# Clearing a stage's semaphores by ranges of numbers instead of one by one

## What is computed

```python
# x: (1, 2048, 256), ctx: (1, 1601, 256)
x = x + L0_xattn(ln(x), ctx, Wq, Wk, Wv, Wo, bo, Wfc, gamma, beta)
x = x + L0_ffn(ln(x), router_w, expert_bias, w1, w3, w2, sw1, sw3, sw2)
x = x + L1_xattn(ln(x), ctx, ...)        # attention both ways and a gate
x = x + L1_ffn(ln(x), gate_W, expert_W, out_W)

# L0_ffn: 8 experts, the 2 best for each token, and 2 shared experts
shared = sum(ffn(xf, sw1[i], sw2[i], sw3[i]) for i in range(2))
rw, sel = top_k(xf @ router_w.T + expert_bias, 2)
rw = softmax(rw)
out = shared + sum(combine[:, e] * ffn(xf, w1[e], w2[e], w3[e]) for e in range(8))
# ffn(x, w1, w2, w3) = (silu(x @ w1.T) * (x @ w3.T)) @ w2.T
```

## Time and profile before

| | us |
|---|---|
| median of 3 runs | 1076.73 |
| lowest and highest | 1076.3, 1080.12 |
| the profiled execution | 1076.45 |
| its span, first to last instruction | 1074.5 |

### The profile page before, as it was taken

One profiled execution on the slowest core, in us unless ns is written; L12 is line 12 of the kernel. 1 busy time (PEld: TensorE's weight loads), 2 busy tenths in 40 slices (PEclk: granted clock), 3 DMA queues, 4 the chain that ended last, 5 costly groups with the idle time before them and its releaser, 6 DMA issues. The chain is left out here.

```text
span 1074.5 us, 18717 instructions
## 1 busy us (share of the span) xinstructions
PE 998.5 (93%) x6840; PEld 919.0 (86%) x6840; DVE 678.7 (63%) x1605; ACT 512.2 (48%) x1041; POOL 404.3 (38%) x636
## 2 busy tenths in 40 slices
PE   4999999599999999999889999999999999999983
PEld 4899998478889999997778799998998999999973
DVE  5567776359668888774675545455445677766662
ACT  4546665233367777772344433333334444444441
POOL 5225544415324343414542100000015867677540
PEclk9999999689999999999998999999999999999995
DMA  7200000021078888863213400000001101111000
GB/s 223 79 1 2 1 2 1 1 79 59 20 229 254 255 250 254 252 210 113 74 40 99 109 1 20 1 1 1 2 1 21 25 21 31 26 31 31 11 10 11
DMA packets 56881, 76.54 MB, mean 71 GB/s; under 512 B 5536, under 2 KB 37408, under 8 KB 56800
## 3 DMA queue, kind: packets, MB, share of 16 engines
q1 hardware_dynamic: 38896, 50.04, 15.7%
q0 software_dynamic: 15648, 22.81, 7.3%
q10 hardware_dynamic: 2256, 2.62, 0.7%
HBM read 61.43 MB, written 14.02 MB: 70 GB/s over the span
## 5 line engine op out<-in xcount | busy, mean ns | idle before, releaser
L43 PE MATMUL bank<-V_hi,XT_lo 128*128 128x256 f32 x416 | 123.6, 297 | 1.4 <-DVE XT_lo L2231 1.4
L2231 DVE TENSOR_TENSOR XT_lo<-bank,XT_lo 128x512 fp32r<-128x512 f32 x116 | 73.3, 633 | 76.3 <-ACT XT_lo L1924 75.8
L1924 ACT ACTIVATE XT_lo<-bank 128x512 fp32r<-128x512 f32 x116 | 63.8, 552 | 118.8 <-PE bank L1683 118.1
L45 PE MATMUL bank<-V_hi,XT_lo 128*128 128x256 f32 x416 | 117.1, 282 | 0.0
L44 PE MATMUL bank<-V_lo,XT_lo 128*128 128x256 f32 x416 | 116.8, 281 | 0.0
L454 DVE TENSOR_TENSOR expert_w_lo<-sraw,expert_w_hi 128x1024 fp32r<-128x1024 f32 x72 | 88.1, 1224 | 32.6 <-ACT expert_w_hi L450 30.2
L2236 DVE TENSOR_REDUCE part<-wide 128x1 f32<-128x402 f32 (+1 forms) x116 | 72.4, 624 | 38.7 <-PE wide L45 36.7
L43 PE MATMUL wide<-expert_w_hi,XT_hi 128*128 128x402 f32 (+1 forms) x232 | 91.5, 394 | 3.4 <-issue 2.4
L45 PE MATMUL wide<-expert_w_hi,XT_hi 128*128 128x402 f32 (+1 forms) x232 | 85.6, 369 | 0.0
L44 PE MATMUL wide<-expert_w_lo,XT_hi 128*128 128x402 f32 (+1 forms) x232 | 85.5, 368 | 0.0
L43 PEld LDWEIGHTS bank<-V_hi,XT_lo 128*128 128x128 f32 x416 | 78.3, 188 | 4.6 <-DVE XT_lo L2231 2.9
(11 more groups left out here) (454 smaller groups left out, 3242.9 us busy)
## 6 DMA issues: line engine op xcount, KB each, us to landing
sraw<-w1T SPq DMA_DIRECT2D x25, 512.0 KB, 5.0
sraw<-w3T SPq DMA_DIRECT2D x25, 512.0 KB, 5.1
sraw<-w2T SPq DMA_DIRECT2D x25, 512.0 KB, 6.9
XT_hi<-queries POOLq DMA_DIRECT2D x16, 256.0 KB, 3.2
routed_results<-rys POOLq DMA_DIRECT2D x15, 256.0 KB
X<-x ACTq DMA_DIRECT2D x4, 512.0 KB, 8.0
token_rows<-Fx SPq DMA_DIRECT2D x4, 512.0 KB, 4.9
out<-X SPq DMA_DIRECT2D x16, 128.0 KB, 1.7
```

The costliest lines, as they stand in the source:

```text
L43: pe.matmul(out, wh, xh, start=first, stop=False)
L45: return pe.matmul(out, wl, xh, start=False, stop=last)
L1924: act.activation(weights(g, nk, 0), transposed(g, nk), ACT.Copy).then_inc(sem["high"], 1)
L2231: dve.tensor_tensor(weights(g, nk, 1), transposed(g, nk), weights(g, nk, 0).bitcast(F32), ALU.subtract).then_inc(sem["low"], 1)
```

## The change

`give_back` is registered once for each stack instead of once for each call of `sems`, gets all semaphores that the stage took, sorts their numbers, and clears each run of consecutive numbers by one instruction. The instruction is the same as before, a clear of a range with a first and a last number; before, first and last were always equal.

```diff
+        taken_by = {}
+
         def sems(ctx, names):
             got = [free_sems.pop(0) for _ in names.split()]
 
-            def give_back():
-                for s in got:
-                    nc.gpsimd.sem_clear(s)
-                free_sems.extend(got)
-            ctx.callback(give_back)
+            def give_back(taken):
+                numbers = sorted(s.num for s in taken)
+                firsts = [n for n in numbers if n - 1 not in numbers]
+                lasts = [n for n in numbers if n + 1 not in numbers]
+                for first, last in zip(firsts, lasts):
+                    nc.gpsimd.sem_clear(range(first, last + 1))
+                free_sems.extend(taken)
+            if ctx not in taken_by:
+                taken_by[ctx] = []
+                ctx.callback(give_back, taken_by[ctx])
+            taken_by[ctx].extend(got)
             return got
```

## The result

The changed kernel takes 1069.19 us (median of 8 runs, 1067.3 to 1075.34), the kernel before 1076.8 us (8 runs on the same chip, 1074.53 to 1080.12). The ratio is 0.9932, with a 95% interval of 0.991 to 0.9953: 7.3 us less, between 5.1 and 9.7. The profiled run of the changed kernel took 1068.18 us.

A forecast was written before the change was run, and what follows sets the result against it. PE was busy 93%, but POOL's clears counted at the end and ahead of the closing stage: 6.0 + 1.92 = 7.9 us off 1076.45 gave 1068.53, predicted as 1068.6 us, range 1067.4 to 1071.6.

The forecast's parts named there:

- The tail: Program's end, where nothing but clears runs: 86 clears become 5, so 81 x 74 ns = 6.0 us leave the span.
- the term for the new instruction: All six places: each range clear costs 74 ns, however long its range; seven of them lie on the path.
- B: Rival at all clears: a clear walks its range at 44 ns a member; gain only 3.2 us, 1073.3 us; chance 0.08.
- The closing stage: Stage after the routed one: 28 clears become 2, POOL starts 1.92 us sooner and everything behind moves by 1.92 us.
- the string: Closing stage: POOL's store, gathers and inverse(0), started at the barrier, set the time of PE's transposes; SHIFT 1.92 us sooner.
- The wait at the transposes: Closing stage: PE's two waits, 3.43 us together, become one of about 1.5 us at the first transposes.
- Everything behind moves by 1.92: Closing stage: all work behind PE's wait at the first transposes comes 1.92 us earlier.
- The other four places: First attention, router, routed and last stages: fewer clears gain 0, with 0.3 us either way.
- A: Rival: the closing stage's gain fails through a slow start behind the barrier or a slipped landing; 1069.4 to 1070.5 us; chance 0.10.
- The sign that I had named for A: Closing stage's first product to the last stage's: 77.7 us forecast; still 79.6 us would mean its gain failed.
- C: Rival at the program's end: other engines' work hides the 6.0 us, only 1.92 remains; 1074.6 us; chance 0.05.
- D: Rival: a range costs above 74 ns a member, so the kernel is slower; 1078.3 us at 88 ns; chance 0.02.

The follow-up runs named there:

- the kernel with two edits: The changed kernel, with the last routed result's store moved to SP's queue and inverse(0) into the middle of the fourth group of gathers: 1067.4 us, ratio 0.9929.

## Why the prediction was right, and where it was off

**The tail: right in kind, 0.4 us too large.** 6.0 us predicted, 5.63 found. The 74 ns per single clear held (and held when doubled). What was off is the term for the new instruction: I took 74 ns each whatever the length, the five take 0.74 us in all instead of 0.37. "A range instruction that walks would be of little use" was the weak sentence: it walks, at 5.3 ns where issuing one more clear costs 74, and is of use all the same. B was right in form and 8 times too dear at 44 ns. The figure that it took from the Trainium skill ("Runtime: NRT & Kernel Launch", section "The ~15µs preamble/postamble breakdown": about 1.5 us for 51 semaphores), 29 ns each by my estimate, fits neither: here the trace has 74 for a clear by itself and 5.3 inside a range, and the measurement decides.

**The closing stage: the string was right, the size nearly at POOL, less so in the stage.** 1.92 us predicted for POOL's start, 1.71 found (the two ranges of 14 take 110 ns each). At SHIFT it was 1.76 in the mean of four against four. The steps up to SHIFT were seen: the store at 0.74 (0.6 to 0.7 predicted), the wait ahead of `result(1, 0)` gone in all four profiles with ranges. The wait at the transposes was not the 1.5 us predicted but 2.1 to 2.4 in three profiles and none in one. In the kernel with ranges in the closing stage alone PE came 1.29 us sooner to the transposes (34.14 against 35.43), where I had reckoned with 1.02, and SHIFT came 1.6 sooner, not 1.92; the difference, 0.6, is the longer wait.

**What the prediction did not have: the clock behind that wait.** "Everything behind moves by 1.92" took the products behind the transposes as fixed. They take 41.4 to 41.7 us or 42.8 to 43.3, by the granted clock, in kernels of both kinds. It fell in two of four profiles with single clears and in three of four with ranges (the fourth had no wait there), too few to say that the change made it more likely. The stage gained 1.4 us in the means, not 1.92, and the 1.4 leans on one profile.

**The other four places: right.** Nothing to be seen with ranges, nothing to be seen with twice the clears. Over the twelve profiles, six with single clears ahead of these stages (one of them with twice the clears) and six with ranges, the means are 166.26 and 166.21 us for the first attention, 81.97 and 82.14 for the router stage, 190.19 and 190.59 for the routed one, 502.58 and 502.98 for the last. Within one kind profiles differ by 0.4 to 4.5 us, so this excludes a gain of the clears' length in the first attention and the router stage, and says less of the other two.

**The sum.** 5.63 + 1.4 to 1.76 = 7.0 to 7.4 us, against 7.3 measured by the ratio (5.1 to 9.7). The gap to the 7.9 predicted is the walk (0.4 + 0.2) and, as far as the profiles go, the clock. That 1068.6 and 1069.19 us lie only 0.6 apart is closer than the runs can tell, and in part luck. Whole times show the tail: ranges at the end alone give a ratio of 0.9952. They don't show the closing stage's part: the changed kernel's ratio of 0.9932 is 2.2 us lower, and the two intervals overlap. Its evidence is the rows of POOL and PE. One figure of the list of signs was a plain slip: the last group was to end "near 1060.5"; by the prediction's own sum it is 1074.5 - 7.9 = 1066.6, and it ended at 1066.1.

**The rivals.** A, a lost start behind the barrier: from the last clear's end to POOL's store are 0.49 us with two range clears ahead as with 28 single ones (0.74 - 0.25 and 2.45 - 1.96), so no start was lost, and this part of A falls. Its other part, a landing that slips, did happen: the second group of gathers began at +12.30 to +13.80 us in the four profiles with ranges. By the rule of the Trainium skill cited with it ("Runtime: NRT & Kernel Launch", section "Instruction fetch mechanics") a taken branch whose target is outside the two pages held waits for a fetch; here fewer clears ahead of the branch made it no longer, and whether the 0.49 us hold a fetch no run shows. The sign that I had named for A was a bad one: a span of 79.6 us from the stage's first product to the next stage's. Three of the four profiles with ranges came within 0.3 us of it (the stages of 79.36 to 79.51), with the store on time: the clock behind the wait and those landings hide the gain in that span. The store's row was the sign to read. C falls with the time around the span, 2.0 us before and 2.1 after, and with the time of the kernel that has ranges at the end alone. D, over 74 ns a member, falls by the rows of 14 to 39 members and that of 140.

## What to carry to other kernels

Work on an engine that is busy 38% can still be worth something at two kinds of place: at the very end, where here it counted in full, and at a barrier where that engine starts a string of steps, each waiting for a landing, on whose last the busy engine waits. There it came through to the end of the string, and only in part, as far as nine profiles can say, to the stage. Look there first for what can be started by an idle queue: one store moved to another queue hid all the clears of that barrier, and with two groups of small operations moved ahead of a landing the closing stage took 75.3 us, in one profile each with single clears and with ranges, where ranges alone had 76.9 to 79.5. And where single profiles of a kernel differ by more than the change is worth, compare stage by stage, counted from a mark of the stage's own, and take several profiles of each.

## What the hardware showed that I had not expected

A clear of a range takes 44 ns for its first member and, in ranges of 14 to 140 members, 5.1 to 5.3 ns for each further one (110 and 784 ns); ranges of 3, 6 and 10 take 46, 66 and 88 ns; clears issued one by one cost 74 ns each, twice or once.

The granted clock fell behind a wait of PE at the transposes in six of the eight profiles that had one: a mean of 0.72 over the next 6 us, part of them at 1.2 GHz. It fell behind all four waits of 2.1 us and behind two of the four of 2.41 us, so the length of the wait doesn't decide it. Where it fell, what follows the transposes took 1.1 to 1.6 us longer. A wait that is made shorter but not taken away may therefore save more or less than its length; what decides the fall stays open.

The first group of gathers landed 8.7 to 10.2 us after it was begun (8.68 in the kernel with two edits), with single clears and with ranges alike. It shares that time with six weight loads on SP's queue. I did not test whether these loads, begun later, would shorten it.
